# Zero rows of the score operands by DMA from a zeroed tile instead of GpSimd memsets, router logits behind the first maxima

## What is computed

```python
x = LN(x + attention(x))          # 16 heads of 16, causal, keys and values through a 128-wide latent,
                                  # plus a 32-wide rotary part that all heads share
x = LN(x + cross(x, memory))      # 77 keys, with a mask
logits = x @ w_router             # 8 experts
gates  = top2(softmax(logits))
out = LN(x + sum(gate[e] * expert_e(x)))   # expert: w2 (silu(w1 x) * (w3 x))
```

## Time and profile before

| | |
|---|---|
| median of 3 executions | 1621.0 us |
| profiled execution | 1616.89 us |
| its span | 1615.2 us |
| mean granted TensorE clock | 0.898 |
| busy: PE, weight load, DVE, ACT, POOL | 1371.1, 959.9, 790.3, 624.1, 359.3 us |
| moved by DMA | 131.80 MB, mean 82 GB/s |

### The profile page before, as it was taken

How to read it: one execution, slowest core, us unless ns; L and a number is a source line. 1 busy time by engine, 2 the same in 40 slices (tenths; PEclk the granted TensorE clock), 3 DMA queues, 4 the chain that set the end, 5 groups by cost and what they waited for, 6 DMA issues and landing times.

```text
span 1615.2 us, 25041 instructions
## 1 busy us (share of the span) xinstructions
PE 1371.1 (85%) x7580; PEld 959.9 (59%) x7581; DVE 790.3 (49%) x1636; ACT 624.1 (39%) x1327; POOL 359.3 (22%) x434
## 2 busy tenths in 40 slices
PE   3688999879899976989988799997359999999980
PEld 2545566655555564655566556555248888888870
DVE  3364452677544386644348655506733333333325
ACT  2124556313455521445642244562423333333324
POOL 5201112210411401131230132110332222222225
PEclk9789999968999996999988699998579999999995
DMA  4752113830321382032156212217311111111119
GB/s 148 205 97 41 29 20 100 199 63 1 87 47 42 118 171 41 12 83 40 43 165 123 40 46 47 40 42 260 105 56 53 49 49 52 52 49 49 52 38 310
DMA packets 87836, 131.80 MB, mean 82 GB/s; under 512 B 14944, under 2 KB 46944, under 8 KB 87584
## 3 DMA queue, kind: packets, MB, share of 16 engines
q1 hardware_dynamic: 74064, 100.98, 26.0%
q0 software_dynamic: 7936, 24.20, 4.6%
q10 hardware_dynamic: 5744, 5.43, 1.1%
HBM read 70.34 MB, written 40.98 MB: 69 GB/s over the span
## 4 chain that ended last, share of the span: by engine, by line
PE 70%; DVE 9%; issue 6%; DMA 6%; POOL 4%; ACT 2%; SPq 2%; ACTq 0%; POOLq 0%; DVEq 0%
PE ps L1089 13%; PE ps L777 11%; PE ps L754 10%; PE ps L778 8%; PE ps L1076 8%; PE ps L792 8%; DMA kas<-scr_k 3%; PE ps L732 3%; PE ps L758 2%; PE ps L1097 2%; DVE nmax L1274 2%; POOL xs L485 1%; PE ps L1059 1%; PE ps L1009 1%; DVE x L1335 1%
## 5 line engine op out<-in xcount | busy, mean ns | idle before, releaser
L1142 ACT ACTIVATE pT<-ps 128x512 f32<-128x512 f32 (+3 forms) x768 | 344.5, 493 | 349.0 <-PE ps L778 348.9
L1274 DVE TENSOR_REDUCE nmax<-ps 128x1 f32<-128x640 f32 (+3 forms) x256 | 258.5, 1024 | 118.6 <-PE ps L758 113.8
L777 PE MATMUL ps<-qs,kas 128*128 128x512 f32 (+2 forms) x768 | 308.7, 410 | 8.9 <-DMA qs<-nmaxT 5.3
L754 PE MATMUL ps<-kas,qs 127*128 127x512 f32 (+2 forms) x768 | 247.8, 412 | 27.1 <-DMA kas<-scr_k 16.2
L778 PE MATMUL ps<-qs,kbs 127*128 127x512 f32 (+2 forms) x768 | 268.0, 357 | 0.0
L777 PEld LDWEIGHTS ps<-qs,kas 128*128 128x128 f32 x768 | 150.2, 196 | 140.8 <-ACT pT L1142 102.2
L472 POOL TENSOR_SCALAR_AFFINE_SELECT pT<-pT 128x512 f32<-128x512 f32 x128 | 81.2, 634 | 661.9 <-ACT pT L1142 661.8
L754 PEld LDWEIGHTS ps<-kas,qs 127*128 127x128 f32 x768 | 152.0, 220 | 62.2 <-issue 12.9
L1271 DVE TENSOR_REDUCE nmax<-ps 128x2 f32<-128x256 f32 (+3 forms) x128 | 104.4, 825 | 151.0 <-PE ps L758 150.1
L792 PE MATMUL ps<-pT,vaug 128*17 128x512 f32 (+3 forms) x1536 | 161.2, 491 | 15.7 <-POOL pT L472 15.6
L778 PEld LDWEIGHTS ps<-qs,kbs 127*128 127x128 f32 x768 | 149.9, 195 | 5.4
(11 more groups left out here) (199 smaller groups left out, 1775.3 us busy)
## 6 DMA issues: line engine op xcount, KB each, us to landing
xb<-xs SPq DMA_DIRECT2D x72, 129.0 KB, 2.1
qs<-rs SPq DMA_DIRECT2D x32, 256.0 KB, 6.1
scr_q<-stg SPq DMA_DIRECT2D x16, 512.0 KB, 2.7
scr_k<-stg SPq DMA_DIRECT2D x16, 512.0 KB, 3.6
kas<-rs SPq DMA_DIRECT2D x32, 256.0 KB, 6.2
qs<-scr_q SPq DMA_DIRECT2D x64, 128.0 KB, 5.4
kas<-scr_k SPq DMA_DIRECT2D x64, 128.0 KB, 6.2
kbs<-scr_k SPq DMA_DIRECT2D x64, 128.0 KB, 4.1
```

Source lines behind the costliest of these rows:

```text
L754: ins = pe.matmul(ps[:, slot + bank, 0:n_k], qs[0:MROW, g % 2, h, i * P:(i + 1) * P], kas[0:MROW, g % 2, h, k0:k0 + n_k], start=True, stop ...
L777: pe.matmul(o, kas[:, g % 2, h, j * P:(j + 1) * P], qs[:, g % 2, h, w0:q1], start=True, stop=False)
L1142: act.activation(pT[:, u % 2, h, 0:q1 - q0], ps[:, s2_bank(n), q0 - w0:q1 - w0], ACT.Exp, scale=ATT_SCALE).then_inc(s_exp, 1)
L1274: dve.tensor_reduce(nmax[:, k:k + 1], ps[:, slot:slot + 2, :].rearrange("p s n -> p (s n)")[:, 0:(i + 1) * P], AX.X, ALU.max, negate=True) ...
```

## The change

1. GpSimd's `zero_keys` (memset of `kas` set 0, in the prologue and at each boundary), its memset of `kbs` at each boundary, and the first memset of `kbs` are removed, with their waits.
2. In `first_groups`, SP gets two DMAs more for each batch: rows 96 to 126 of `kas` set 0 from the same rows of `qs` set 0 (which stay zero from the start on), between the ones and the last two saves; and the same rows of `kbs`, between its rotary rows and its low part. PE waits for these DMAs.
3. The logits' matmuls stand behind all units of `first_maxima`.
4. ACT takes the exponential of the logits in the next batch, behind the first four exponentials of its scores.
5. `ALONE_AT`, `COUNT_AT` and `PAIRED_AT` put maximum units of group 1, and the counts, later among the score units.

```diff
-ALONE_AT = (0, 1, 3, 5, 7, 10, 12, 14)
+ALONE_AT = (0, 5, 6, 8, 10, 13, 15, 17)
-COUNT_AT, PAIRED_AT = 9, 15
+COUNT_AT, PAIRED_AT = 12, 18
...
-                pool.memset(kbs[KROWS:MROW, :, :].bitcast(F32), 0.0).then_inc(s_zl, 1)
-                pool.wait_ge(s_zl, 1)
...
-                def zero_keys(b):
-
-                    pool.wait_ge(s_pr, b * N_PROJ + QK[3] + 1)
-                    pool.sem_inc(s_seen, 1)
-                    pool.wait_ge(s_rs, b * 4 + 4)
-                    pool.sem_inc(s_seen, 1)
-                    pool.memset(kas[KROWS:MROW, 0, :, :].bitcast(F32), 0.0).then_inc(s_zk, 1)
-                    pool.wait_ge(s_zk, b + 1)
-                    pool.sem_inc(s_seen, 1)
...
-                zero_keys(0)
...
-                    if then:
-                        pool.wait_ge(s_tri, (b + 1) * NG * len(DIAG))
-                        pool.sem_inc(s_seen, 1)
-                        zero_keys(b + 1)
...
-                        pool.memset(kbs[KROWS:MROW, :, :].bitcast(F32), 0.0).then_inc(s_zl, 1)
...
                     place_ones(0)
+                    if first:
+                        sp.wait_ge(s_zero, 1)
+                    sp.dma_start(kas[KROWS:MROW, 0, :, :].bitcast(F32), qs[KROWS:MROW, 0, :, :].bitcast(F32)).then_inc(s_zk, 16)
                     for m in range(6, 8):
                         save_part(b, m)
...
                     place_rope(kbs, 3, s_kb)
+                    sp.dma_start(kbs[KROWS:MROW, :, :].bitcast(F32), qs[KROWS:MROW, 0, :, :].bitcast(F32)).then_inc(s_zl, 16)
                     for h in range(2):
                         load_klow(b, 0, h)
...
-                        pe.wait_ge(s_zk, b + 1)
+                        pe.wait_ge(s_zk, b * 16 + 16)
...
-                            pe.wait_ge(s_zl, b + 1)
+                            pe.wait_ge(s_zl, b * 16 + 16)
...
-                    fill(12, 13, 14)
+                    fill(*range(12, N_S1))
                     for hf in range(2):
                         pe.wait_ge(s_t8r, b * NT + 4 * hf + 4)
...
-                    fill(*range(15, N_S1))
...
+                def gates(b):
+                    act.wait_ge(s_le, b + 1)
+                    act.activation(lg[:, 1, :, :], lg[:, 0, :, :], ACT.Exp).then_inc(s_lex, 1)
...
+                            if ahead and g == 0 and u == 0:
+                                gates(b - 1)
```

More of the change, by code:

```diff
@@ L527, in batch @@
                     power(1, 1, s_ve2, s_pow2)
[L528 to L532, removed]
-                        pool.memset(kbs[KROWS:MROW, :, :].bitcast(F32), 0.0).then_inc(s_zl, 1)
-                        pool.wait_ge(s_zl, b + 2)
-                        pool.sem_inc(s_seen, 1)
                 batch(0, True, False)
@@ L1130, in proj, with batch @@
                                        proj_bank(u, first).rearrange("p (t h d) -> p t h d", t=2, h=NH), ACT.Copy).then_inc(s_vc, 1)
-                def batch(b, then):
+                def gates(b):
+                    act.wait_ge(s_le, b + 1)
+                    act.activation(lg[:, 1, :, :], lg[:, 0, :, :], ACT.Exp).then_inc(s_lex, 1)
+                def batch(b, then, ahead):
                     for g in range(NG):
@@ L1179, in batch @@
                     act.activation(x2b[:, :, 0:D], x2[:, :, 0:D], ACT.Copy).then_inc(s_x2b, 1)
-                    act.wait_ge(s_le, b + 1)
-                    act.activation(lg[:, 1, :, :], lg[:, 0, :, :], ACT.Exp).then_inc(s_lex, 1)
                 for u in range(N_PROJ):
                     proj(0, u, True)
-                batch(0, True)
+                batch(0, True, False)
                 with act.Fori(1, B - 1) as b:
-                    batch(b, True)
-                batch(B - 1, False)
+                    batch(b, True, True)
+                batch(B - 1, False, True)
+                gates(B - 1)
                 act.wait_ge(s_x, (B + 1) * 16)
```

## The result

The changed kernel takes 1700.7 us (median, 1697.46 to 1704.88) against 1624.19 for the kernel before, measured beside it: ratio 1.0465, interval 1.0424 to 1.0506, so **76.5 us slower**. The forecast was 1688.0, in a range of 1640 to 1800. The profiled execution has a span of 1699.4 us against 1615.2.

A forecast was written before the change was run, and what follows sets the result against it. PE was taken to set the time for 70% of the span, with DVE, GpSimd, DMA and issue for the rest. Prologue 37.6, boundaries 27.3 and gates 3 sum to 67.9; 1621.0 + 67 = 1688 us, range 1640 to 1800.

The forecast's parts named there:

- Z: Price of one 31-row zero transfer on SP's queue, carried by one DMA engine: 20.3 us, eight such transfers.
- the fast share: Rate taken for the one engine carrying the 31 rows: 410 GB/s / 16 = 25.6 GB/s, 19.8 us a transfer.
- The slow share: Rival: the one engine carries the 31 rows at 12.9 GB/s, 39.4 us a transfer; 1840 us, chance 0.08.
- The order of the ring: On SP's queue, each engine works in order, so everything issued behind a 31-row transfer lands later by its whole price.
- The third rival: On SP's queue, later transfers' entries pass the 31-row one, so only its two semaphores count: 1640 us, chance 0.11.
- Prologue: Before the first scores, both zero transfers delay PE, less 3 us of slack and time given back: +37.6 us.
- Boundaries: Between batches: late `kas` loads and low parts outweigh gains from norm and logits: +9.9, +7.5, +9.9, together +27.3 us.
- Gates and constants: In the score stages, later exponential of the logits, picks and group 1 units cost about 1 us a batch: +3.
- The second rival: The 31-row transfers are spread over the engines like their neighbours, 2.6 us each: -11.7, 1609 us, chance 0.11.
- 4.4 for the logits: In the spread-transfer case, gain from logits filling PE's wait of 1.70 to 2.1 us at the boundaries, twice: -4.4.
- 31 has no equal shares: Argument against spreading: 31 rows have no divisor up to 16, so one engine takes the whole transfer.
- The median: Step from profiled execution (1616.9 us) to median of the runs, 4 us above it: 1621.0 + 67 = 1688.

The follow-up runs named there:

- act_dma: `pool_dma` with the 31 `kas` rows issued from ScalarE's queue instead of GpSimd's: ratio 1.0135 to the kernel before.
- split16: The changed kernel with each 31-row transfer cut into 16 and 15 rows: 1612.5 us against 1626.1 for the kernel before, ratio 0.9916.
- pool_dma: Kernel before, with the boundaries' zeros as 31-row transfers from GpSimd's queue and logits behind the first maxima; prologue memsets kept: 1594.9 us, ratio 0.9797.

## Why the prediction was right

- **Z.** Forecast 20.3 us: one engine at the fast share of 25.6 GB/s and half a microsecond. The 31 packets take 21.3 us in the prologue, 27 GB/s in all but the first four, and PE's start in the prologue moved by 20.9 us against one profile of before and by 20.0 against the mean of two. The saves took 24.0 us to land, and 7.2 when the zeros ahead of them were spread. Right in mechanism and size. The slow share (12.9 GB/s, Z = 39.4) is seen only where others are at work beside the engine: the first four packets took 0.8 to 1.5 us, the rest 0.61.
- **The order of the ring.** Right, and for the reason given. Traffic of 68.4 to 84.2 us, between the first rows and the last, and of 84.2 to 87 us:

```profile
DMA packets 26, 0.43 MB, mean 27 GB/s; under 512 B 0, under 2 KB 0, under 8 KB 0
...
DMA packets 35, 0.07 MB, mean 23 GB/s; under 512 B 3, under 2 KB 3, under 8 KB 35
```

  The saves were issued at 62.24, and the other engines had done their shares by 68.4. Until 84.2 there isn't one small packet: the busy engine does rows and nothing else. Then come the saves' 32 packets of 2 KB, two times 16, with three of a few bytes, and the saves have landed. It is the same behind `kbs`' zeros, whose rows run up to 140.2 us (traffic of 140.2 to 141.6):

```profile
DMA packets 24, 0.03 MB, mean 24 GB/s; under 512 B 6, under 2 KB 8, under 8 KB 24
```

  These are the low parts' last packets and the maxima's. The view of the low parts could mislead here (from issue to landing min/median/max):

```profile
DMA to landing us min/median/max: 15.5/24.3/33.1
```

  Two low parts share a semaphore, and the view takes the first as landed at the sixteenth count, whichever of the two it comes from; both had the last of their counts only from 140.9 us on. PE waited there for the zeros themselves (19.87 us, `DMA kbs<-qs`, in the timeline of after above) and for the maxima's transfer, issued at 121.20 with 20.86 to run. The third rival (the engine is shared, the ring isn't held) is thus wrong for one queue. Engines take packets in turn only between queues, as `act_dma` shows, and even there it didn't help.
- **Prologue.** Forecast +37.6, measured +37.7. By parts: up to PE's first maxima 20.3 against 20.0, from there to the scores 17.3 against 17.7.
- **Boundaries.** Forecast first maxima +10.6, measured +12.3 in the mean of the gaps. From there to the scores -0.7, -3.1 and -0.7, measured -3.3, -3.0 and -1.4. Together +27.3 against +29.3. The late saves set the first, and in the second the logits grew to 6.83 us, which the norm (4.74 to 1.38) and their new place more than paid.
- **Gates and constants.** Forecast +3, read as +7 (the two groups of profiles) to +10 (the change against before): this is the term that was too small, the bulk of the 9 us between 67.9 and 76.5. The wait that the estimate had in mind, 1 us a batch, is about what the 33rd score unit shows (1.0 and 1.5); it left out what comes later in the stages and in batch 0, whose cause stays open.
- **The second rival** (a spread transfer, 1609 us, -11.7 against before) was then built: `split16` measured -13.6. Part of that agreement is luck, since its terms were off both ways: prologue +7.9 against +5, boundaries -29.1 against -22.7, score stages +10.6 against +6. (Its 4.4 for the logits is also more than two waits of 1.70 to 2.1 make.) "31 has no equal shares" holds on SP's and ScalarE's queues; on GpSimd's it doesn't.
- **The median.** The sum was made against 1616.9 and set on 1621.0; beside the changed kernel the one before had 1624.2. The difference, 76.5, is what to lay beside 67.9; the forecast time of 1688 is 12.7 low, 3.2 of it for the median and 0.9 for rounding 67.9 to 67.

## What to carry to other kernels

Count the rows of a transfer before its bytes: on the queues of SP and ScalarE, 31 rows cost more than 16 and 15 together (21 us of packets against landings in 5.5 and 7.0), and the loss appears in whatever stands behind, and beside it on the other's queue; so look at the aggregate rate (one engine's 27 GB/s) before blaming the transfer that PE waits for. A memset that stops DVE for 3.5 us is worth replacing, but only where the replacement isn't ahead of what PE waits for next: here the prologue wanted the memset and the boundaries the transfer. And a stage of one profile is not a baseline: two profiles of the same kernel differed here by up to 4 us a stage and 14 us in all.

## What the runs showed of the hardware

- 31 rows of 16 KB from SP's queue: 27 GB/s, 21.3 us from the first packet to the last; from GpSimd's queue: landed in 6.0 us. The same shape, source and destination. `pool_dma` had been expected to hide 20 us, not to need 6.
- One DMA engine does the packets of one queue in order: 26 of 16 KB without a small one between them, then the 32 of 2 KB that were issued behind. Between SP's and ScalarE's queues it alternates: 17 of 16 KB and 18 small ones in 12 us.
- The same 32 logits matmuls take 3.86 us in one place and 6.83 in another, 14 us later at the same boundary: granted clock 0.94 in the middle of the maxima, 0.50 behind them.
- GpSimd's memset of 3.51 us stretched DVE's `keep` to 3.40 us; while GpSimd issues a transfer, `keep` takes 0.47.
